# Attention with the maximum subtracted in SBUF, exponentials taken out of the PSUM of the transposes, and scores of two heads as a pair of 48-row matmuls

## The chip, the cores and the metric

One Trainium2 chip, one core. The metric is the time on the device in microseconds, the median over several runs. The traces shown are of one profiled execution each.

## What is computed

A transformer layer over a batch of 8 with 512 positions and 256 channels, all in float32: cross attention from `x` to `ctx` with 16 heads of 16 channels, an additive bias of 512 x 512 that all heads and batches share, and a padding mask; then a feed-forward layer whose weights and activations are rounded block by block to FP4.

```python
q = (query @ w_q.T + b_q).reshape(B, T, H, D)            # query = layernorm(x)
k = (key @ w_k.T + b_k).reshape(B, S, H, D)              # key = value = ctx
v = (value @ w_v.T + b_v).reshape(B, S, H, D)
scores = jnp.einsum('bthd,bshd->bhts', q * SCALING, k) + attn_bias[None]
scores = jnp.where(key_padding_mask[:, None, None, :], NEG_INF, scores)
attn = jax.nn.softmax(scores, axis=-1)
out = jnp.einsum('bhts,bshd->bthd', attn, v).reshape(B, T, E)
x = x + (out @ out_proj_w.T + out_proj_b)
gate = fp4_linear(layernorm(x), w_gate); y = fp4_linear(layernorm(x), w_up)
x = x + fp4_linear(jax.nn.silu(gate) * y, w_down)
```

## The kernel before, in words

The attention is cut into tiles of 128 queries x 512 keys of one head. A batch has 64 tiles, in two octets (periods) of 8 heads; all batches together have 512. The order of the work on each engine is written out by hand: `body(b)` issues a batch, the first and the last batch are unrolled and the others run in a hardware loop, and the engines meet through semaphores only.

A tile passes these stations:

- TensorE makes the scores (L1099). Query and key are split into a high and a low part in fp32r, so that a full-precision product is a single matmul with 128 contraction rows: `stack` holds high and low parts of two heads on top of each other. One head of the pair is zeroed in the query by `parity4`. The scores go to one of three PSUM banks; the matmul waits until VectorE has emptied the bank (`biased`).
- VectorE adds bias and mask, copies to `prob` in SBUF, and takes the row maximum (L845, `neg_max`).
- ScalarE takes the exponential in SBUF with the maximum as its bias and sums the row (L569).
- TensorE transposes the four 128 x 128 blocks (L967, `transpose_prob`) six tiles later, into one of three other banks.
- VectorE (L764, even tiles) or ScalarE (L608, odd tiles) copies the transposed tile to `probT`.
- TensorE multiplies with the values (L1056, `values`): four heads at once in four column groups of 32, eight instructions for one chunk of 128 keys, after every second tile on average.
- The sums are inverted, expanded on GpSimd (L445), transposed (`make_r`, L1002), copied (L614), and multiplied into the output (L733).

Between the tiles TensorE also makes q, k, v and the output projection (L982, L988, L995, L1013) for the next octet or the batch before, and transposes of `xn` and `ctx`. The SP queue copies high and low parts into `stack`, 32 DMAs for each octet (L367, L378), reloads the bias for every batch (L407), and loads the feed-forward weights in the last batch. These weights are quantised in nine pieces during the last batch by VectorE (L808 to L823), GpSimd (L484 to L493), TensorE (L1027, L1030) and ScalarE (L592 to L597). The feed-forward layer then runs over 32 row tiles (L1217 to L1245), after a start in which the last output projection is made. It isn't changed.

## Time and profile before

| | |
|---|---|
| median of 3 runs | 1028.66 us (1028.31 to 1029.89) |
| the profiled execution | 1029.46 us, its span 1027.5 us |
| granted TensorE clock, mean | 0.983 |
| instructions | 23032 |
| PE, DVE, ACT, POOL busy | 93%, 83%, 70%, 19% |

PE is TensorE's matmuls, PEld its weight loads, DVE VectorE, ACT ScalarE, POOL GpSimd, SP the queue that issues the DMAs. The profiled execution took 1.96 us more than its span, and 0.80 us more than the median. A view of the chain follows the work that ended last backwards and gives each piece only the time that nothing earlier covers.

### The profile page before, as it was taken

How to read it: one execution, taken by the hardware profiler on the slowest of the kernel's cores; microseconds unless marked ns; L12 is line 12 of the kernel's file. 1: busy time of each engine (PE TensorE's matmuls, PEld its weight loads, DVE VectorE, ACT ScalarE, POOL GpSimd, SP SyncE). 2: the span in 40 equal slices, each digit the busy share in tenths (PEclk: the TensorE clock that was granted, in tenths of full speed). 3: DMA queues.
4: the chain of work that ended last, by engine and by line, in shares of the span. 5: the costliest groups of instructions: out<-in, count | busy, mean ns of one | idle time of the engine just before them, and what ended most of it. 6: DMA issues, size and time to landing. Idle time of an engine off the chain costs nothing.

```text
span 1027.5 us, 23032 instructions
## 1 busy us (share of the span) xinstructions
PE 952.6 (93%) x6612; PEld 667.7 (65%) x6612; DVE 857.5 (83%) x2125; ACT 722.0 (70%) x1685; POOL 198.6 (19%) x156
## 2 busy tenths in 40 slices
PE   5299999999999999999999999978778999999997
PEld 3176666666657666665765766645456878878885
DVE  3287988888888888888888878899757999999996
ACT  2298988877888888888788888856634555555542
POOL 3222232140240213114024121245400000000000
PEclk9699999999999999999999999999979999999999
DMA  9553451451533335055153433611000000000000
GB/s 290 134 124 76 113 124 27 121 138 28 120 101 90 84 103 123 15 129 132 36 115 93 103 75 89 145 35 31 2 0 6 17 16 15 21 16 15 20 16 26
DMA packets 47339, 76.14 MB, mean 74 GB/s; under 512 B 10016, under 2 KB 26784, under 8 KB 47264
## 3 DMA queue, kind: packets, MB, share of 16 engines
q1 hardware_dynamic: 47264, 75.34, 29.3%
q8 instruction: 22, 0.36, 0.2%
q14 instruction: 53, 0.43, 0.2%
HBM read 20.78 MB, written 4.19 MB: 24 GB/s over the span
## 4 chain that ended last, share of the span: by engine, by line
PE 82%; DVE 8%; issue 5%; SPq 2%; ACT 2%; DMA 1%; DVEq 1%; POOL 0%; ACTq 0%; POOLq 0%
PE psum L967 24%; PE psum L1099 14%; PE psum L1056 12%; PE psum L1235 9%; PE psum L1217 4%; PE psum L1219 4%; PE psum L1218 4%; PE psum L988 3%; PE psum L995 3%; PE psum L1013 2%; PE psum L982 2%; DVE att L845 2%; DVE att L764 2%; SPq L367 1%; SPq L378 1%
## 5 line engine op out<-in xcount | busy, mean ns | idle before, releaser
L569 ACT ACTIVATE att<-att,neg_max 128x512 f32<-128x512 f32 x512 | 367.3, 719 | 119.1 <-DVE neg_max L845 111.9
L845 DVE CUSTOM_DVE_ANT_0 att<-psum,att 128x512 f32<-128x512 f32 x512 | 346.7, 686 | 106.2 <-PE psum L1099 94.2
L967 PE MATMUL psum<-ident,att 128*128 128x128 f32 x2448 | 364.7, 275 | 19.9 <-DVE att L764 7.4
L967 PEld LDWEIGHTS psum<-ident,att 128*128 128x128 f32 x2448 | 298.0, 141 | 94.6 <-issue 45.6
L1099 PE MATMUL psum<-stack 128*128 128x512 f32 x512 | 273.1, 535 | 26.4 <-DMA stack<-kl 17.3
L1099 PEld LDWEIGHTS psum<-stack 128*128 128x128 f32 x512 | 96.7, 189 | 141.4 <-DVE neg_max L845 81.3
L764 DVE COPY att<-psum 128x512 f32<-128x512 f32 x256 | 175.6, 686 | 3.7 <-PE psum L967 3.7
L1056 PE MATMUL psum<-att 128*32 128x256 f32 x2048 | 164.0, 393 | 2.0 <-issue 2.0
L608 ACT ACTIVATE att<-psum 128x512 f32<-128x512 f32 x256 | 150.5, 588 | 18.1 <-PE psum L967 13.1
L1235 PE MATMUL psum<-att 128*128 128x256 f32 (+1 forms) x384 | 98.0, 388 | 2.8 <-ACT att L649 2.8
L569 ACT ACTIVATION_READ_ACCUMULATOR att<-att,neg_max 128x1 f32 x512 | 96.9, 189 | 0.0
L1217 PE MATMUL psum<-stack,qh 128*128 128x512 f32 (+1 forms) x192 | 76.6, 399 | 7.7 <-DVE att L899 7.2
L1235 PEld LDWEIGHTS psum<-att 128*128 128x128 f32 (+1 forms) x384 | 65.7, 189 | 20.1 <-issue 10.6
L654 ACT ACTIVATE att<-psum 128x704 f32<-128x704 f32 x32 | 24.4, 762 | 73.4 <-PE psum L1219 73.4
L473 POOL TENSOR_TENSOR att<-att 128x512 f32<-128x512 f32 x32 | 40.2, 1281 | 179.3 <-DMA att<-in_fside_1xSxS_dram 179.3
L1219 PE MATMUL psum<-stack,ql 128*128 128x512 f32 (+1 forms) x192 | 73.5, 383 | 0.0
L1218 PE MATMUL psum<-stack,qh 128*128 128x512 f32 (+1 forms) x192 | 73.3, 382 | 0.0
L1056 PEld LDWEIGHTS psum<-att 128*32 128x32 f32 x2048 | 40.9, 108 | 45.1 <-issue 43.5
L1217 PEld LDWEIGHTS psum<-stack,qh 128*128 128x128 f32 x192 | 37.2, 194 | 16.6 <-issue 9.0
L464 POOL TENSOR_TENSOR ql<-att,qh 128x1024 fp32r<-128x1024 f32 x16 | 38.0, 2375 | 27.8 <-DVE qh L705 27.7
L845 DVE DVE_READ_ACCUMULATOR2_ANT neg_max<- 128x1 f32 x512 | 42.6, 83 | 0.0
L1218 PEld LDWEIGHTS psum<-stack,qh 128*128 128x128 f32 x192 | 37.4, 195 | 5.8
(96 smaller groups left out, 1043.7 us busy)
## 6 DMA issues: line engine op xcount, KB each, us to landing
stack<-qh SPq DMA_DIRECT2D x128, 128.0 KB, 2.4
stack<-ql SPq DMA_DIRECT2D x128, 128.0 KB, 2.3
att<-in_fside_1xSxS_dram SPq DMA_DIRECT2D x16, 512.0 KB, 3.7
stack<-kh SPq DMA_DIRECT2D x128, 64.0 KB, 2.0
stack<-kl SPq DMA_DIRECT2D x128, 64.0 KB, 2.0
att<-in_ctx_dram SPq DMA_DIRECT2D x8, 512.0 KB, 4.8
out_dram<-att SPq DMA_DIRECT2D x32, 128.0 KB, 1.7
x<-in_x_dram SPq DMA_DIRECT2D x1, 3584.0 KB, 20.4
```

Source lines behind the costliest of these rows:

```text
L473: pool.tensor_tensor(bias_m[:, tt, :], bias_m[:, tt, :], mask_neg, ALU.add).then_inc(bias_ready, 1)
L569: act.activation(prob[:, slot, :], prob[:, slot, :], ACT.Exp, bias=neg_max[:, slot:slot + 1], scale=-1.0, accum_out=row_sum[:, o, tt * 8 + ...
L608: act.activation(probT[:, u % 2, k, :, (tt % 2) * P:(tt % 2) * P + P], ps_T[:, bank_of(jm)[0], :].rearrange("p (c t) -> p c t", c=SC), ACT ...
L764: dve.tensor_copy(probT[:, u % 2, k, :, (tt % 2) * P:(tt % 2) * P + P], ps_T[:, bank_of(jm)[0], :].rearrange("p (c t) -> p c t", c=SC)).th ...
L845: dve.tensor_tensor_reduce(out=prob[:, slot, :], in0=ps_score[:, bank_of(j)[0], :], in1=bias_m[:, tt, :], scale=-1.0, scalar=BIG, op0=ALU. ...
L967: return pe.transpose(out_, in_, ident[:, :])
L1056: last = pe.matmul(ps_O[32 * k:32 * k + 32, half * 2 * P:(half + 1) * 2 * P], vpad[:, o, c, 2 * k + r, :], probT[:, u % 2, k, c, :], start ...
L1099: pe.matmul(ps_score[:, bank, :], q_stack[o][:, k, r, tt * P:(tt + 1) * P], k_stack[o][:, k, :], start=True, stop=True).then_inc(score_rea ...
L1217: pe.matmul(ps_gu[:, c0:c1], f_xqT_high[:, par, c, :], w_gu_high[:, c, c0:c1], start=c == 0, stop=False)
L1218: pe.matmul(ps_gu[:, c0:c1], f_xqT_high[:, par, c, :], w_gu_low[:, c, c0:c1], start=False, stop=False)
L1219: last = pe.matmul(ps_gu[:, c0:c1], f_xqT_low[:, par, c, :], w_gu_high[:, c, c0:c1], start=False, stop=c == EC - 1)
L1235: last = pe.matmul(ps_y[:, 1 - par, :], f_hqT[0:rows, 1 - par, c, :], w_dnT[0:rows, c, :], start=c == 0, stop=c == IC - 1)
```

## The change

The attention is rewritten; the feed-forward loop stays.

- A step is now two tiles, of two heads (r = 0, 1), and `stack` holds 48 rows for each head: high, high, low of the query against high, low, high of the key (`planes_q`, `planes_k`). The 48-row matmuls of a pair stand at rows 0 and 64 of the array. The rows get there through a DRAM tensor, `qk_planes`: 6 DMAs write the planes of an octet and 8 read them, where 32 copied within SBUF.
- The exponential no longer reads `prob`. GpSimd (`less_max`, L548) subtracts the maximum from 20 of the 32 tiles of an octet, ScalarE (L682) from the other 12. The tile is then transposed, and ScalarE's exponential is the copy out of PSUM (L675) for every tile. VectorE has no copy out any more, and no row sums are read.
- The transposes have two banks, one for each r, where they had three, and start four steps (8 tiles) after the scores.
- The sums come from a column of ones beside each head's 16 values (`vv`). The output is copied (`take_O`), transposed to queries in rows (`make_ot`), divided (`normalise`), and transposed back (`make_oT`).
- q, k, v and the output projection are issued in pieces of 256 columns, one a step (`heavy`); transposes stand at the end of a step (`light`).
- The weights' pieces begin with `w_down`; VectorE's work on them starts in step 2 of the last batch's 32 instead of at tile 22 of its 64.

```diff
+        N_OCT = 2 * B
+        STEPS = 16
+        TILES = 2 * STEPS
+        T_LAG = 4
+        V_LAG = 8
+        RING = 16
+        VW = D + 1
...
+        ps_score, ps_O = psum[:, 0:3, :], psum[:, 6, :]
+        ps_T = (psum[:, 3, :], psum[:, 7, :])
+        M0, M1 = psum[:, 4, :], psum[:, 5, :]
...
+        def by_act(s, r):
+            return r == 1 and s % 4 != 0
...
+            def less_max(n, s, r):
+
+
+                slot = (2 * s + r) % RING
+                pool.wait_ge(biased, TILES * n + 2 * s + r + 1)
+                pool.tensor_tensor(prob[:, slot, :], prob[:, slot, :], neg_max[:, slot:slot + 1].to_broadcast([P, S]),
+                                   ALU.subtract).then_inc(less_pool, 1)
...
-                    act.activation(prob[:, slot, :], prob[:, slot, :], ACT.Exp, bias=neg_max[:, slot:slot + 1], scale=-1.0,
-                                   accum_out=row_sum[:, o, tt * 8 + 2 * k + r:tt * 8 + 2 * k + r + 1]).then_inc(exp_ready, 1)
...
+                act.activation(probT[:, u % 2, 2 * kk + r, :, (tt % 2) * P:(tt % 2 + 1) * P], ps_T[r].rearrange("p (c t) -> p c t", c=SC),
+                               ACT.Exp, scale=1.0 if by_act(s, r) else -1.0).then_inc(exp_ready, 1)
...
-                    pe.matmul(ps_score[:, bank, :], q_stack[o][:, k, r, tt * P:(tt + 1) * P], k_stack[o][:, k, :],
-                              start=True, stop=True).then_inc(score_ready, 1)
...
+                for r in range(2):
+                    rows = slice(64 * r, 64 * r + 48)
+                    pe.matmul(ps_score[:, SCORE_BANK[2 * S_ + r], :], q_stack[rows, 2 * o + h, kk, tt * P:(tt + 1) * P],
+                              k_stack[rows, 2 * o + h, kk, :], start=True, stop=True).then_inc(score_ready, 1)
...
+                t = TILES * n + 2 * s + r
+                wait(pe, exp_ready, t - 1)
+                pe.wait_ge(less_act if by_act(s, r) else less_pool, taken_off(n, s, r))
...
+                for S_ in range(2 * STEPS):
+                    scores(b, S_)
+                    transpose_tile(b, S_, 0)
+                    heavy(b, S_, 0)
+                    transpose_tile(b, S_, 1)
+                    values(b, S_)
+                    heavy(b, S_, 1)
+                    light(b, S_)
```

TensorE, in the middle of a batch, before: scores (L1099) of one tile, transposes (L967) of another, and a group of values (L1056) after every second tile.

```order
L1056 MATMUL psum<-att 32x256 x4
L260 REGISTER_ALU
L1099 MATMUL psum<-stack 128x512
L260 REGISTER_ALU
L967 MATMUL psum<-ident,att 128x128 x4
L260 REGISTER_ALU
L1099 MATMUL psum<-stack 128x512
L967 MATMUL psum<-ident,att 128x128 x4
L1056 MATMUL psum<-att 32x256 x4
```

The same place in the change: the pair of scores (L1178), transposes (L1085) of two tiles with a piece of the output projection (L1140) between them, the values (L1214), and at the end of some steps four more transposes.

```order
L1178 MATMUL psum<-stack 128x512 x2
L1188 REGISTER_ALU
L1085 MATMUL psum<-ident,att 128x128 x4
L1140 MATMUL psum<-att 128x256
L1188 REGISTER_ALU
L1085 MATMUL psum<-ident,att 128x128 x4
L1214 MATMUL psum<-att 32x256 x4
L1124 REGISTER_ALU
L1085 MATMUL psum<-ident,att 128x128 x4
L270 REGISTER_ALU x2
```

The two scores of a step moved together and are followed by transposes at once; the number of transposes and of value matmuls for two tiles is the same.

The SP queue, from the load of the rest of `x` to the first octet's operands, before:

```order
L336 DMA x<-in_x_dram 128x28x256
L367 DMA stack<-qh 32x1024 x8
L367 DMA stack<-ql 32x1024 x8
L378 DMA stack<-kh 32x512 x8
L378 DMA stack<-kl 32x512 x8
```

And in the change, where the first four of the eight loads of `stack` are enough for the first eight steps:

```order
L373 DMA x<-in_x_dram 128x28x256
L399 DMA qk_planes<-k_hl 8x16x512 x3
L399 DMA qk_planes<-q_hl 8x16x512 x3
L421 DMA stack<-qk_planes 48x2x512 x8
L399 DMA qk_planes<-q_hl 8x16x512 x3
```

32 issues became 14, and the loads wait for the planes to have been written.

GpSimd in the last batch of the change: a piece of the weights is three instructions (L555, L557, L560) between those of `less_max` (L548).

```order
L548 TENSOR_TENSOR att<-att,neg_max 128x512 x3
L555 TENSOR_TENSOR att<-att 128x512
L557 TENSOR_TENSOR att<-att 128x512
L560 TENSOR_TENSOR att<-att 128x512
L548 TENSOR_TENSOR att<-att,neg_max 128x512 x2
```

The pieces stood alone there before; now tiles of the attention queue behind them.

## Rows read from the trace of the kernel before

**Rows 1.** The page: busy time of each engine, share of the span, instructions

```profile
PE 952.6 (93%) x6612; PEld 667.7 (65%) x6612; DVE 857.5 (83%) x2125; ACT 722.0 (70%) x1685; POOL 198.6 (19%) x156
```

**Rows 2.** Stages: start:end, length, busy PE, PEld, DVE, ACT, POOL, granted clock

```profile
204.63:290.70 86.07, 84.74 (x672) 56.39 (x664) 72.31 (x196) 72.26 (x174) 20.63 (x15) 1.00 0.38 93
635.10:735.30 100.20, 85.03 (x649) 53.99 (x649) 93.21 (x246) 71.13 (x169) 42.49 (x35) 1.00 0.23 59
735.30:748.30 13.00, 10.21 (x101) 5.51 (x99) 5.08 (x14) 6.60 (x16) 1.92 (x2) 0.92 0.01 1
748.30:788.60 40.30, 28.17 (x111) 22.41 (x110) 27.04 (x66) 15.66 (x32) 1.29 (x2) 0.82 0.00 1
```

**Rows 3.** Chain within a middle batch: start, own time, engine, target, line

```profile
413.70 0.24 PE psum L1099
413.94 0.44 PE psum L967 x4
414.38 0.57 PE psum L1056 x8
414.95 0.43 PE psum L1099
...
417.49 0.59 PE psum L967 x4
...
421.72 0.87 PE psum L1013 x4
```

**Rows 4.** Chain within the feed-forward loop, from one down projection to the transposes

```profile
819.91 1.30 PE psum L1235 x6
...
821.33 1.49 PE psum L1235 x6
822.82 0.81 PE psum L967 x6
```

**Rows 5.** PE, 800 to 1000, by shape: busy, mean ns, idle before

```profile
L1235 PE MATMUL psum<-att 64*128 64x256 f32 x50 | 17.4, 428 | 0.0
```

**Rows 6.** Chain at the loop's turn to its next batch

```profile
204.63 2.03 issue
```

**Rows 7.** Groups of one middle batch, by shape: busy, mean ns, idle before, releasers

```profile
L569 ACT ACTIVATE att<-att,neg_max 128x512 f32<-128x512 f32 x64 | 45.9, 719 | 11.4 <-DVE neg_max L845 10.5
L845 DVE CUSTOM_DVE_ANT_0 att<-psum,att 128x512 f32<-128x512 f32 x64 | 43.4, 686 | 12.2 <-PE psum L1099 10.5 <-issue 0.6
...
L608 ACT ACTIVATE att<-psum 128x512 f32<-128x512 f32 x33 | 19.4, 588 | 2.1 <-PE psum L967 1.4
...
L473 POOL TENSOR_TENSOR att<-att 128x512 f32<-128x512 f32 x4 | 5.0, 1284 | 24.7 <-DMA att<-in_fside_1xSxS_dram 24.7
```

**Rows 8.** Timeline of the start: start, duration, engine, line

```profile
20.75 5.06 SPq L367 DMA_DIRECT2D stack<-qh  x8
...
36.08 4.95 SPq L378 DMA_DIRECT2D stack<-kl  x8
...
42.57 1.19 PE L1099 MATMUL psum<-stack 128*128 128x512 f32 x2 [17.34 <-DMA stack<-kl]
```

**Rows 9.** DMA issues, 18 to 42: KB each, us to landing

```profile
stack<-qh SPq DMA_DIRECT2D x8, 128.0 KB, 5.4
```

**Rows 10.** Waits in the last batch: total us, times, longest

```profile
PEld psum L1099 <- DVE neg_max L845: 17.0, 26, 2.3
```

**Rows 11.** Chain near the end of the last batch

```profile
728.79 0.47 DVE stack L796
...
729.86 0.60 DVE att L845
```

**Rows 12.** GpSimd, 635 to 750, by shape: busy, mean ns, idle before

```profile
L486 POOL TENSOR_TENSOR att<-att 128x512 f32<-128x512 f32 x9 | 11.5, 1281 | 0.7
```

**Rows 13.** Timeline of ScalarE where the feed-forward layer starts

```profile
745.47 0.60 ACT L614 ACTIVATE att<-psum 128x512 f32<-128x512 f32 x1 [2.44 <-PE psum L967]
745.96 0.50 ACT L636 ACTIVATE att<-x,neg_mean 128x256 f32<-128x256 f32 x1
```

More of the change, by code:

```diff
@@ L48, in xattn_ffn @@
     SC = S // P
-    TILES = 32
-    UNIT = 8
     ROWS = B * NT
@@ new lines, in planes_free, with bias_again @@
+            def planes_free(o, loads):
+                for h in range(2):
+                    sp.wait_ge(stacked[2 * o + h], 64 * loads)
+                    plain(sp)
+            planes_k(0)
+            planes_q(0)
+            stack_octet(0, 0)
+            planes_free(0, 1)
+            planes_q(1)
+            def bias_again(b, tt):
+                sp.wait_ge(biased, b * 2 * TILES + TILES + 2 * (8 + 2 * tt + 2))
+                plain(sp)
+                sp.dma_start(bias_m[:, tt, :], bias_v[:, tt, :]).then_inc(bias_in[tt], 16)
@@ new lines, in make_tc, with make_qk @@
+            def make_tc(bp, i, bank):
+                pe.wait_ge(ctx_in, 16 * (bp + 1))
+                for tt in range(NT):
+                    last = transposes(bank[:, tt * P:(tt + 1) * P], ctx_n[:, tt, i * P:(i + 1) * P])
+                last.then_inc(tc_ready, 1)
+            def make_qk(which, o, piece, bank, ready):
+                h, c = piece // 2, piece % 2
+                src = (xnT, ctxT)[which]
+                cols = slice(h * 2 * P, (h + 1) * 2 * P)
+                last = pe.matmul(bank[:, cols], w_inT[:, c, which * E + o * P:which * E + (o + 1) * P], src[:, c, cols],
+                                 start=c == 0, stop=c == EC - 1)
+                if piece == 3:
+                    last.then_inc(ready, 1)
@@ L998, in make_v, with make_ot @@
+            def make_v(i, piece, bank):
+                x, c = piece // 2, piece % 2
+                s = 2 * i + x
+                last = pe.matmul(bank[:, x * E:(x + 1) * E], ctxT[:, c, s * P:(s + 1) * P], w_inT[:, c, 2 * E:3 * E],
+                                 start=c == 0, stop=c == EC - 1)
+                if piece == 3:
                     last.then_inc(v_ready, 1)
-            def make_r(n):
-                pe.wait_ge(inv_ready, n + 1)
+            def make_ot(quad, bank):
+                pe.wait_ge(O_taken, quad + 1)
@@ new lines, in make_ot, with make_oT, make_out @@
+                last.then_inc(ot_ready, 1)
+            def make_oT(m, o, bank):
+                pe.wait_ge(ot_taken, 2 * m + 2)
+                for tt in range(NT):
+                    last = transposes(bank[:, tt * P:(tt + 1) * P], O_n[:, tt, o * P:(o + 1) * P])
+                last.then_inc(oT_ready, 1)
+            def make_out(i, piece, bank):
+                x, c = piece // 2, piece % 2
+                tt = 2 * i + x
+                last = pe.matmul(bank[:, x * E:(x + 1) * E], oT[:, c, tt * P:(tt + 1) * P], w_outT[:, c, :],
+                                 start=c == 0, stop=c == EC - 1)
+                if piece == 3:
@@ L1196, in step @@
+            batches(pe, body)
+            for S_ in range(V_LAG):
+                transpose_tile(B, S_, 0) if S_ < T_LAG else None
+                transpose_tile(B, S_, 1) if S_ < T_LAG else None
+                values(B, S_)
+                if S_ == 2:
+                    weights_free(8)
+                    make_ot(4 * B - 2, M1)
             def step(n, par):
```

1139 lines of the change are left out of this document (609 added, 530 removed).

## The prediction

> **What bounds the kernel now.** The page comes first: PE is busy 93% of the span, DVE 83%, ACT 70%, POOL 19% [rows 1]. That is an average, so the stages come next. Six middle batches take 86.0 to 86.3 us each, and in one of them PE is busy 84.7 of 86.07 us, DVE and ACT 72.3 [rows 2]. The last batch takes 100.2 us with PE busy only 85.0 and DVE 93.2. Then 13.0 us of drain, and 40.3 us of a start of the feed-forward layer in which PE is busy 28.2 [rows 2]. The first scores start at 42.57 [rows 8].
>
> For the middle batch I read the chain, because it gives each piece its own price. Four transposes cost 0.44 us, a group of values 0.57, a score matmul 0.24 if transposes stand ahead of it and 0.43 if values do. Four transposes behind values cost 0.59 instead of 0.44, and two 256-column projection pieces 0.87 [rows 3]. So two tiles cost 0.24 + 0.44 + 0.43 + 0.44 + 0.57 = 2.12 us, and 32 such pairs 67.8. Projections (32 pieces of 0.435) add 13.9, 24 other transposes at 0.11 add 2.6, and the turn of the loop 2.0 [rows 6]: 86.3 against 86.07 measured. TensorE's order of instructions explains the middle batches by itself. DVE, ACT and POOL are not what is paid for there, however much the change relieves them.
>
> **What a middle batch costs then.** The copy by DVE, the row sums and the exponential in SBUF go. By the prices above they were hidden under PE: 72.3 of 86 us on DVE and ACT. So I cost their removal at nothing, and look at PE alone.
>
> - The pair of scores. Half of the array's rows serve each head. If the two run side by side, the pair costs one matmul behind values: 0.43. No row shows such a pair. The nearest is a group of values: eight instructions in four column groups cost 0.57, much less than eight times a 256-column piece's 0.22 [rows 3]. From that I take the pair as one. The other bound is a second matmul of 0.24.
> - The switch of shape. The pair has 64-row tiles, the transposes behind it the full array. Two rows price this. Six down matmuls of which two have 64 rows cost 1.49 against 1.30, and the six transposes behind them 0.81 against 6 x 0.11 = 0.66 [rows 3 to 5]. So a switch costs 0.15 to 0.19, as 0.59 against 0.44 does behind values. I add 0.15 to the first transposes of each step; the switch in front of the pair is in the 0.43.
> - A step is then 0.43 + 0.59 + 0.44 + 0.57 = 2.03, against 2.12 for the same two tiles. I use 2.04 for the second start.
>
> In the Trainium skill, "TensorEngine Tiling (Array Packing)", section Tiling Modes, changing the tiling mode drains the TensorE, and the 0.15 to 0.19 of the rows agree. By "TensorE: Matmul & The Clock Gate", Part 3, matmuls in different row groups start about 4 ns apart; taken alone that would make the pair one matmul, and no row here shows it.
>
> 32 steps make 65.3. Projections stay at 13.9. Other transposes rise from 24 to 40 (outputs there and back, no sums): 4.4. Ten groups of them stand behind values, with a switch each: 1.5. With the loop's 2.0 the batch costs 87.1, against 86.3 by the same prices: +0.8, or **+5 us** for six batches. The saving on scores is paid out again for switches and transposes.
>
> Are the others fast enough? ACT takes 64 exponentials out of PSUM, from 0.50 (a plain copy's 588 ns less overlap) to 0.62 (the exponential's 719) each, 24 subtractions at 0.62 and 15 copies at 0.5: 54 to 62 of 87 us [rows 7]. POOL subtracts 40 tiles at 1.28, 51 us, plus about 17 for its other work (20.6 now, less the expansions of the sums) [rows 2]: 68. DVE keeps 64 score operations at 0.60 [rows 7, 11] and 14 us of small work (72.3 now, less 64 and 32 operations at 0.60): 52. All have room.
>
> **The start: -10.5 us.** Now 32 issues follow each other from 20.75 to 41.0, 0.63 each, and the first score waits for the last [rows 8]. Then it is six plane writes, whose last issue falls at about 22; a landing of up to 5.4 us beside the load of `x` [rows 9], giving 26 to 27; four loads of `stack` at 0.63, 2.5 us; and 3 us to land, between the 1.5 from the last issue to the first score now [rows 8] and 5.4. First score at about 32; with 5.4 for both landings 35, with 1.5 for both 28.
>
> **The first batch: 0.** It has fewer transposes and values in both kernels. Its first steps are paced by DVE at 1.2 us and more instead of PE; a like excess is in the batch now.
>
> **The last batch: -11 us.** PE without waits: 32 x 2.04 = 65.3, eight value pieces and eight output pieces 7.0, 60 transposes 6.5, 15 switches 2.3: 81. Now it waits 17.0 us for DVE [rows 10], as the weights and the copies meet there. The copies go (32 at 0.60, 19 us), so DVE's sum falls from 93 to 74 to 78. But steps 18 to 28 hold two weight operations each, at 0.47 to 0.60 and more [rows 11], beside 1.2 us of scores, two take-outs and two divisions: about 35 us against 27 on PE, with three score banks and so little lead. That costs 8. POOL is as close: 40 tiles and nine pieces of 3 x 1.28 [rows 12] and small work make 89 to 92 us, of which four steps of lead (9 us) hide most. 81 + 8 = 89 against 100.2.
>
> **Drain and hand-over: +2 us.** Four steps of transposes and values at 1.6 and four of values at 0.45, with the last exponentials: 10 against 13.0 [rows 2]: -3. But ACT may begin the feed-forward layer only after the copy of the last output, while it begins now at 745.96, 2.3 us before the last values end [rows 13]; and the last octet goes through transposes there and back with a copy each (0.44 + 0.6) before its projection: +5.
>
> **The sum**: -10.5 + 0 + 5 - 11 - 3 + 5 = -14.5. Against the profiled execution's 1029.5 (span 1027.5 and 2 around it) that is 1015; that execution lies 0.8 over the median of 1028.66, so 1014.2, I say 1014. The profit per step that decides is small: 14.5 / 256 = 0.057 us. Any price over that on the pair turns the sign.
>
> **The rivals.**
> - The pair runs one after the other. Then each step costs 0.21 to 0.24 more on PE, 54 us for 256 steps, of which the last batch's waits take in 6: 1062, slower. Against it speaks the group of values, in columns only. Chance 0.10.
> - The pair runs side by side, but its second weights (128 columns) load after the first. A load not covered by a matmul shows as 0.43 instead of 0.24, drain and load together, so at most 0.11: 28 us, 1042, slower. Chance 0.08.
> - Two transpose banks are too few. A bank is free only when ACT has done its exponential, with a subtraction of 0.62 and perhaps a copy ahead of it. From T_ready I get about 0.5 + 0.62 + 0.67 = 1.8 us plus the hops, and the next transposes into the bank come 2.04 later, or 2.47 where a projection piece is between. In 28 of 32 steps there is one. If every step still lost 0.07 to 0.1, it would be 2.4 a batch: 19 us, 1033. Chance 0.10.
> - The switch to the pair and back costs nothing extra. 256 x 0.15 = 38 less: 976. The rows with 64-row tiles speak against it. Chance 0.06.
> - The sum holds: 0.66, with a range of its own from 1000 to 1028 (start ±3, last batch -4 to +8, middle batches ±0.8 each, hand-over ±3).
>
> **How the numbers follow.** The time is that of the sum. From 990 to 1044 lie the last case's range, the third case, nearly all of the second, and what lies between: 0.8. A measurement of this kernel tells 0.2%, 2 us, from no change. Faster than 1026.6: 0.61 of the 0.66, all of the fourth case's 0.06, and 0.03 of the third: 0.70. Within 0.2%: 0.05. Slower: 0.25.
>
> **What would show it.** In the changed trace: the two score matmuls start within some 10 ns, and the chain has about 0.43 for both; transposes behind them at 0.59, not 0.44; a middle batch at 86 to 88 us with PE busy nearly all of it; the first score near 32; VectorE's share of the middle batches near 60%; a last batch near 89, with waits for DVE and POOL. Score matmuls 0.2 apart would make the prediction wrong, and so would PE waiting for the exponential in ordinary steps.

## The result, and the profile after

The changed kernel takes **1049.87 us** (median of 4 runs, 1044.90 to 1052.12), the kernel before 1029.28 beside it (1028.31 to 1031.17): a ratio of 1.0191, 95% interval 1.0152 to 1.0231. It is slower, by 1.9%. I had forecast 1014 and "faster" at 0.70; the time lies outside my range of 990 to 1044 as well. The profiled execution is the slowest of the four, 2.25 us over the median, so the sum by stages below explains 22.7 us of span where the medians differ by 20.6.

The page of the changed kernel, whose profiled execution took 1052.12 us (compare [rows 1]; the columns are those of the page):

```profile
span 1050.2 us, 22498 instructions
PE 965.9 (92%) x6740; PEld 651.1 (62%) x6740; DVE 725.6 (69%) x1897; ACT 604.7 (58%) x1125; POOL 501.1 (48%) x478
...
L675 ACT ACTIVATE att<-psum 128x512 f32<-128x512 f32 x512 | 303.7, 597 | 258.4 <-PE psum L1085 257.8
L548 POOL TENSOR_TENSOR att<-att,neg_max 128x512 f32<-128x512 f32 x320 | 338.9, 1066 | 233.0 <-DVE neg_max L949 230.6
L1085 PE MATMUL psum<-ident,att 128*128 128x128 f32 (+1 forms) x2576 | 406.8, 285 | 18.6 <-DMA att<-in_ctx_dram 13.9
```

The work moved as planned: VectorE has 132 us less, ScalarE 117 less, GpSimd 302 more, TensorE 13 more. Nothing there looks like 22.7 us of span. So the stages again: start:end, length, busy time (and number) of PE, PEld, DVE, ACT and POOL, granted clock, DMA share, GB/s. The borders are the first score of each batch, the last score step, and the first matmul of the feed-forward layer.

```profile
0.00:39.35 39.35, 12.92 (x66) 11.53 (x66) 7.31 (x18) 7.33 (x11) 14.44 (x22) 0.83 0.83 250
39.35:126.36 87.01, 79.09 (x558) 47.74 (x558) 53.22 (x164) 50.35 (x90) 56.23 (x54) 0.90 0.46 100
126.36:211.78 85.42, 84.92 (x686) 53.25 (x682) 54.06 (x167) 57.75 (x104) 57.82 (x56) 1.00 0.42 94
211.78:301.78 90.00, 86.55 (x684) 54.24 (x680) 54.45 (x167) 57.73 (x104) 57.84 (x56) 0.98 0.40 89
573.58:658.85 85.27, 84.93 (x685) 53.25 (x681) 50.23 (x155) 57.75 (x104) 54.19 (x52) 1.00 0.41 95
658.85:753.75 94.90, 80.94 (x650) 49.62 (x647) 88.48 (x216) 54.91 (x101) 81.63 (x72) 0.98 0.21 55
753.75:772.14 18.39, 12.01 (x122) 7.18 (x123) 5.66 (x18) 11.13 (x22) 4.01 (x4) 0.95 0.00 1
```

Of the six middle batches the first and the last take 85.4 and 85.3 us, and the second 90.0; the three left out, of the same kind as the second, take 89.7 to 91.1. What these four have and the two don't is a turn of the loop (the branch back to the start of its body), which falls between their first and their second step on TensorE. The sum against the trace of before, by the same borders (first scores there at 42.57, 119.41 and 634.19, last step at 734.95, feed-forward layer from 750.82): start -3.2, first batch 87.0 against 76.8, +10.2 (the batch ahead of the loop); the six middle batches 532.5 against 514.8, +17.7; last batch 94.9 against 100.8, -5.9; drain and hand-over 18.4 against 15.9, +2.5; the rest +1.4. That is +22.7.

### The profile page after: what moved, and what is told of

The parts are those of the page before. It is cut to its first block and busy times, and to the rows that moved or that the text cites. A ratio compares the mean times of both kernels' runs of the same rounds, so it can differ in the third digit from the quotient of the medians.

```text
span 1050.2 us, 22498 instructions
## 1 busy us (share of the span) xinstructions
PE 965.9 (92%) x6740; PEld 651.1 (62%) x6740; DVE 725.6 (69%) x1897; ACT 604.7 (58%) x1125; POOL 501.1 (48%) x478
## 5 line engine op out<-in xcount | busy, mean ns | idle before, releaser
L675 ACT ACTIVATE att<-psum 128x512 f32<-128x512 f32 x512 | 303.7, 597 | 258.4 <-PE psum L1085 257.8
L548 POOL TENSOR_TENSOR att<-att,neg_max 128x512 f32<-128x512 f32 x320 | 338.9, 1066 | 233.0 <-DVE neg_max L949 230.6
L1085 PE MATMUL psum<-ident,att 128*128 128x128 f32 (+1 forms) x2576 | 406.8, 285 | 18.6 <-DMA att<-in_ctx_dram 13.9
L1085 PEld LDWEIGHTS psum<-ident,att 128*128 128x128 f32 (+1 forms) x2576 | 295.1, 143 | 146.0 <-issue 88.4
L1178 PE MATMUL psum<-stack 48*128 48x512 f32 x512 | 131.2, 508 | 40.1 <-DVE neg_max L949 22.9
L1214 PE MATMUL psum<-att 128*32 128x256 f32 x2048 | 164.9, 395 | 0.2 <-ACT att L675 0.2
L682 ACT ACTIVATE att<-att,neg_max 128x512 f32<-128x512 f32 x192 | 138.0, 719 | 22.7 <-DVE neg_max L949 22.7
L1178 PEld LDWEIGHTS psum<-stack 48*128 48x128 f32 x512 | 49.3, 187 | 128.4 <-DVE neg_max L949 66.9
L1417 PE MATMUL psum<-stack,q_hl 128*128 128x512 f32 (+1 forms) x192 | 76.3, 397 | 7.1 <-DVE att L1015 7.0
L1107 PE MATMUL psum<-att 128*128 128x256 f32 x256 | 76.1, 388 | 1.0 <-DVE att L930 1.0
L1419 PE MATMUL psum<-stack,q_hl 128*128 128x512 f32 (+1 forms) x192 | 73.4, 382 | 0.0
L1418 PE MATMUL psum<-w_gu_low,q_hl 128*128 128x512 f32 (+1 forms) x192 | 73.2, 381 | 0.0
L1214 PEld LDWEIGHTS psum<-att 128*32 128x32 f32 x2048 | 40.8, 108 | 44.2 <-issue 38.4
L1417 PEld LDWEIGHTS psum<-stack,q_hl 128*128 128x128 f32 x192 | 37.2, 194 | 16.0 <-issue 8.1
L1117 PE MATMUL psum<-att 128*128 128x256 f32 x128 | 42.9, 420 | 0.0
L1418 PEld LDWEIGHTS psum<-w_gu_low,q_hl 128*128 128x128 f32 x192 | 37.2, 194 | 5.7
## 6 DMA issues: line engine op xcount, KB each, us to landing
x<-in_x_dram SPq DMA_DIRECT2D x1, 3584.0 KB, 17.7
```

The source lines that it names most:

```text
L548: pool.tensor_tensor(prob[:, slot, :], prob[:, slot, :], neg_max[:, slot:slot + 1].to_broadcast([P, S]), ALU.subtract).then_inc(less_pool, 1)
L675: act.activation(probT[:, u % 2, 2 * kk + r, :, (tt % 2) * P:(tt % 2 + 1) * P], ps_T[r].rearrange("p (c t) -> p c t", c=SC), ACT.Exp, scal ...
L682: act.activation(prob[:, slot, :], prob[:, slot, :], ACT.Identity, bias=neg_max[:, slot:slot + 1], scale=-1.0).then_inc(less_act, 1)
L1085: return pe.transpose(out_, in_, ident[:, :])
L1107: last = pe.matmul(bank[:, cols], w_inT[:, c, which * E + o * P:which * E + (o + 1) * P], src[:, c, cols], start=c == 0, stop=c == EC - 1)
L1178: pe.matmul(ps_score[:, SCORE_BANK[2 * S_ + r], :], q_stack[rows, 2 * o + h, kk, tt * P:(tt + 1) * P], k_stack[rows, 2 * o + h, kk, :], st ...
```

## The experiments

**Is the pair side by side?** The timeline of TensorE in a middle batch of the changed kernel: start, duration to the end of the last of a group, line, name, number.

```profile
301.45 0.40 PE L1214 MATMUL psum<-att 128*32 128x256 f32 x4
301.78 0.50 PE L1178 MATMUL psum<-stack 48*128 48x512 f32 x2
302.21 0.66 PE L1085 MATMUL psum<-ident,att 128*128 128x128 f32 x4
302.71 0.60 PE L1117 MATMUL psum<-att 128*128 128x256 f32 x2
```

Two score matmuls of 512 columns, and the transposes follow 0.43 us behind the start of the first. The two of a pair start 3 to 4 ns apart, in all 256 pairs of the trace. The run that parts them (`e8_unpaired`):

```diff
...
-                    scores(b, S_)
+                    scores(b, S_, 0)
                     transpose_tile(b, S_, 0)
+                    scores(b, S_, 1)
                     heavy(b, S_, 0)
```

> The changed kernel with the second score matmul of each pair moved behind the first four transposes: the same instructions, not side by side any more. My theory (side by side, the second matmul of a pair costs 4 ns; alone it costs 0.43 behind transposes with a switch of shape there and 0.15 back, less 0.0 hidden): each step rises from 2.04 to about 2.5 or 2.6, 256 steps of 0.5 make 120 to 148 us, about 1170 to 1200. The pair-serial rival: the same matmul costs the same wherever it stands, and only the two switches of 0.15 are added: 77 us or less, below 1127.

1172.26 us (1.1381, 1.1362 to 1.1400). A middle batch takes 104.41 us with PE busy for all of it, 19.1 more than 85.27, or 0.60 a step. In its timeline the single score stands 0.42 to 0.43 ahead of what follows:

```profile
302.96 0.66 PE L1085 MATMUL psum<-ident,att 128*128 128x128 f32 x4
303.55 0.49 PE L1178 MATMUL psum<-stack 48*128 48x512 f32 x1
303.97 0.70 PE L1140 MATMUL psum<-att 128*128 128x256 f32 x2
304.51 0.60 PE L1085 MATMUL psum<-ident,att 128*128 128x128 f32 x4
```

From start to start, the second score takes 0.42, the transposes ahead of it 0.59 instead of 0.50, and the piece of projection behind it 0.54 instead of 0.43: in this step 0.42 for the matmul itself and 0.2 for the two extra changes of shape. One matmul and a pair cost the same, so the first rival (one after the other) and the second (weights that load late) are out.

**The turn of the loop.** First without any loop (`e1_unroll`, the edit shown), and the same in the kernel before (`e2_before_unroll`):

```diff
-            body(0)
-            with eng.Fori(1, B - 2) as b:
+            for b in range(B):
                 body(b)
-            body(B - 2)
-            body(B - 1)
```

> The changed kernel with its loop over the middle batches written out: eight bodies in a row, no branch, nothing else. In its trace the batches with a loop turn behind them take 89.7 to 91.1 us and the two without one 85.3 and 85.4. Theory A (the turn of the loop is what the middle batches lose: VectorE stands 5.6 us there, TensorE 3 us behind it, and the granted clock then falls to half for some us): every middle batch near 85.4, no stretch at half clock between 75 us and the last batch, so five times 4.6 to 5.7 less: 23 to 28 us off 1049.9, about 1024. Theory B (the steps themselves cost more, and the turn only shows where it adds up): the loop's own 2 us go five times, 10 us, about 1040. Rival C (the turn's loss is a data wait that stays without a branch): less than 5 us off.

> The control: the kernel before with its loop written out in the same way. There VectorE stands 2.9 us at the turn and the clock stays at full speed, and the batches with a turn differ from the one without by 2.0 us. Both theories: about six times 2.0, 12 us off 1029, about 1018. If it gains as much as the changed kernel does from the same edit (some 25 us), the turn isn't what makes the changed kernel slower; if it gains 10 to 12, then the turn accounts for about 13 us of the 20 between the kernels.

The changed kernel took 1034.56 us (1.0040, 1.0016 to 1.0064; 1028.05 to 1038.27), 15 less and between the two theories; the kernel before 1018.29 (0.9896, 0.9873 to 0.9919), 11 less. The loops have four and five turns, not the five and six that I had counted. One middle batch of each, the changed kernel first:

```profile
295.10:380.37 85.27, 84.93 (x684) 53.29 (x680) 53.88 (x167) 57.67 (x104) 57.78 (x56) 1.00 0.41 94
```

```profile
202.84:286.96 84.12, 84.12 (x665) 56.38 (x665) 72.18 (x196) 72.55 (x174) 20.96 (x16) 1.00 0.40 96
```

All six are alike to 0.02 us in either kernel. This parts two effects: the steps cost 1.15 us more a batch (I had 0.8), 6.9 in all; and a turn costs 1.9 to 2.2 in the kernel before (five turns, 10.1 us), 4.4 to 5.8 in the changed one (four turns, 20.7). The trace of before shows its turn too, if each batch is counted from its first score: the first middle batch, with no turn ahead of it, takes 84.07 us, the other five 86.03 to 86.30. The profiled execution is 24 us shorter than that with the loop; the median gained only 15. The profiled one with the loop was the slowest of its four, the one without it the fastest of its ten, and those ten fall into two groups: four of 1028.05 to 1029.35 with mean clocks of 0.975 to 0.978, six of 1034.29 to 1038.27 with 0.964 to 0.970. Why isn't settled.

At the turn VectorE stands still. Its timeline in the changed kernel: the last operation ahead of the turn, and the first behind it.

```profile
301.27 0.08 DVE L949 DVE_READ_ACCUMULATOR2_ANT neg_max<- 128x1 f32 x1
306.61 0.69 DVE L949 CUSTOM_DVE_ANT_0 att<-psum,att 128x512 f32<-128x512 f32 x1 [5.26 <-issue]
```

SP had issued three plane writes 2 to 4 us ahead, and TensorE's next scores wait:

```profile
297.03 2.13 SPq L399 DMA_DIRECT2D qk_planes<-q_hl  x3
...
307.37 0.80 PE L1178 MATMUL psum<-stack 48*128 48x512 f32 x2 [3.05 <-DVE neg_max L949]
```

And then the clock is down, by stretches of 3 us (columns as above):

```profile
304.00:307.00 3.00, 0.31 (x8) 0.00 (x0) 0.39 (x1) 1.18 (x3) 0.00 (x0) 0.87 0.16 55
307.00:310.00 3.00, 2.63 (x9) 1.91 (x10) 2.49 (x8) 0.60 (x1) 2.61 (x3) 0.50 0.00 0
310.00:313.00 3.00, 3.00 (x17) 1.42 (x16) 0.32 (x2) 0.60 (x1) 3.00 (x3) 0.50 0.32 69
313.00:316.00 3.00, 3.00 (x26) 1.91 (x25) 1.31 (x4) 1.69 (x3) 1.11 (x2) 0.99 0.51 193
```

After 3 us in which TensorE stood, it is granted 0.50 (1.2 instead of 2.4 GHz) for 6 us of work. The four turns differ in this: TensorE stood 2.6 to 3.05 us at each, and the granted clock was 0.50 for 6.8 us at the two whose batches take 91.1 us, for 3.4 us at the two of 89.7 and 90.0. The kernel before has a clock of 1.00 in all its middle batches.

**Do the plane writes do it?** Two runs move them behind the turn. In `e3_planes_after_turn`:

```diff
-            planes_free(0, 1)
-            planes_q(1)
...
             def body(b):
+                sp.wait_ge(biased, b * 2 * TILES + 4)
...
+                planes_free(0, b + 1)
+                planes_q(2 * b + 1)
...
                     bias_again(b, 2)
-                    planes_free(0, b + 2)
-                    planes_q(2 * b + 3)
                     bias_again(b, 3)
```

> The changed kernel keeps its loop, but the three writes of the query planes (256 KB each) that it issues at the end of a body, 2 to 4 us ahead of the turn, are issued early in the next body. Theory A1 (VectorE's fetch of its instructions after the branch lands late because it stands beside these writes and the loads around them): VectorE's stand at the turn falls from 5.6 us to the 2.9 of the kernel before or less, the clock stays up, and the batches with a turn come to 87 to 88: 10 to 18 us off, 1032 to 1040. Rival A2 (the stand is the longer body's own: more code to fetch, whatever the transfers do): 5.6 us stay, the time stays within 3 us of 1049.9, or it gets worse if the second half's planes then come late.

1083.98 us (1.0529, 1.0494 to 1.0564), 34 slower than the changed kernel, where I had expected 10 to 18 less. Its waits of TensorE in one batch name what took the place of the turn:

```profile
PE psum L1084 <- DMA att<-in_ctx_dram: 4.2, 1, 4.2
```

TensorE's gap at the turn is down to 0.2 to 0.5 us, with as long a body as before; but SP now comes to the context load only 22.6 us into the batch, behind the plane writes and eight stack loads; TensorE stands for it 3.2 to 4.4 us in each of these batches. They take 91.4 to 92.6 us, and the last one 103.7. `e5_planes_and_ctx` puts the context load first in the body, ahead of `planes_q`.

> The changed kernel with its loop, where the next context load, in every batch but the last, is the first transfer that SP issues in a body, and the query plane writes come behind it instead of ahead of the turn. In the run that moved the plane writes alone, the gap of TensorE at the turn was gone (no stand over 1 us there, 2.8 to 3.4 us before), and one of 3.8 to 4.4 us for the context load stood in its place about 28 us into each batch. Theory A1 (two places in SP's queue that exclude each other: plane writes ahead of the turn delay VectorE's instructions, plane writes behind it delay the context tile): with the context load ahead both stands go, batches with a turn take 87 to 88, the first one 79 to 81: 18 to 24 us off 1049.9, 1026 to 1032. Rival (the context tile is late because the stacks and planes keep the DMA engines busy, wherever it is queued): a stand of 2 us or more stays in each batch and the time stays above 1045.

1032.45 us (1.0038, 1.0021 to 1.0056). The loop is still there, and the turn has nearly no price, 0.4 to 0.6 us: here 85.84 us against 85.27 unrolled.

```profile
289.51:375.35 85.84, 85.00 (x685) 53.24 (x682) 54.58 (x167) 57.67 (x104) 57.77 (x56) 1.00 0.39 93
632.08:734.24 102.16, 82.67 (x650) 50.46 (x647) 89.28 (x216) 54.92 (x101) 81.42 (x72) 0.95 0.22 56
```

The last batch pays 7.3 us back: the feed-forward weights come behind the plane writes in the queue, and VectorE waits for the first of them:

```profile
DVE att L908 <- DMA att<-in_L_ffn_w_down_dram: 7.6, 1, 7.6
```

**Traffic, or the order of waits?** Transfers of no use are put back at the old place, in the kernel of `e5_planes_and_ctx` (`e13_copies_at_turn` with three, `e16_six_copies` with six) and in the kernel before (`e14_before_copies` with three, `e17_before_six` with six):

```diff
+                for i in range(3):
+                    sp.dma_start(copy_no[i], bias_v[:, i, :]).then_inc(copied, 16)
```

> The changed kernel with the context load first and the plane writes after the turn (that run: 1032.45, batches with a turn 85.7 to 85.8), and in addition three transfers of 256 KB each at the place where the plane writes had stood, 3 to 4 us ahead of VectorE's branch. They copy rows of the bias in DRAM to a spare DRAM tensor that nothing reads. Theory A1 (transfers in flight when VectorE branches delay its instruction fetch): its stand at the turn is back at 4 us or more, TensorE stands 1.5 us or more, and batches with a turn take 88 to 91: 10 to 25 us slower than without the copies. Rival (the stand came from the order of waits around the plane writes, not from traffic): batches stay at 85.7 to 86.3 and the time within 3 us of 1032.45.

> The kernel before with the same three copies in each batch but the last, issued about 3 us ahead of its turn. There VectorE stands 2.7 us at a turn and the batches take 86.0 to 86.3, against 84.1 without a turn. Theory A1: the stand rises to 4.5 us or more and the six batches with a turn to 88 to 91, the clock falls there too: 10 to 25 us slower than 1029. Rival: unchanged within 3 us.

1033.98 and 1034.61 us (1.0061, 1.0036 to 1.0087; 1.0054, 1.0034 to 1.0073). The first is the rival's number, 1.5 us more than without copies; the second, 5.8 us over the kernel before, is neither's (VectorE stands 3.4 to 4.2 us at its turns instead of 2.5 to 2.7). But in the changed kernel three copies, from DRAM to DRAM, are soon over: in the turn where VectorE's last operation ends at 289.67 us, the DMA view has 0.01 MB from 289.6 to 290.4. Behind the last operation in the changed kernel it has 0.56 MB from 301.4 to 304.3. So twice as many copies:

> As the run with three copies ahead of the turn in the changed kernel (context load first, plane writes after the turn; 1033.98 there, 1032.45 without copies), but with six. Refined theory A1 (the instruction packets come when the data queued ahead has passed): the first packet comes at 3 to 4.5 us behind the branch, VectorE stands 4.0 us or more instead of 1.9 to 2.7, TensorE 1.5 us or more, and batches with a turn take 88 to 91: 1041 to 1055. Rival: the stand stays below 3 us and the time within 4 us of 1034.

> As the run with three copies ahead of the turn in the kernel before (1034.61; VectorE stood 2.9 to 3.7 us at its turns instead of 2.0 to 2.2), but with six. Theory A1: first packet at 3 to 5 us behind the branch, a stand of 4.5 to 6 us, batches of 89 to 92 and a clock that falls at some turns: 1043 to 1065. Rival: below 1037.

1048.13 us (1.0170, 1.0153 to 1.0187) and 1041.83 (1.0106, 1.0088 to 1.0123); the batches with a turn take 87.7 to 91.5 and 88.0 to 88.6, the second kernel a little under what I expected. Copies that nobody needs bring the loss back: by the medians 15.7 us over the run without them in the changed kernel, 11.7 in the kernel before (13.6 and 10.9 by the ratios). The half clock comes back with them in both kernels: it is granted for 3.4 us behind every turn of the kernel before, where without copies it never was. VectorE's turn with six copies in the changed kernel, and the turn without any (`e5_planes_and_ctx`) behind it:

```profile
292.76 0.08 DVE L962 DVE_READ_ACCUMULATOR2_ANT neg_max<- 128x1 f32 x1
297.21 0.69 DVE L962 CUSTOM_DVE_ANT_0 att<-psum,att 128x512 f32<-128x512 f32 x1 [4.36 <-issue]
```

```profile
289.00 0.08 DVE L952 DVE_READ_ACCUMULATOR2_ANT neg_max<- 128x1 f32 x1
291.63 0.69 DVE L952 CUSTOM_DVE_ANT_0 att<-psum,att 128x512 f32<-128x512 f32 x1 [2.55 <-PE psum L1088]
```

The DMA view of these turns (queue: packets, MB, share of 16 engines) says what is late: the first packet of q14, a queue that carries instructions. In the changed kernel, from 300.6 to 304.3 us there are only data, and from 304.3 to 304.8 comes the packet:

```profile
q1 hardware_dynamic: 374, 0.70, 62.0%
```

```profile
q1 hardware_dynamic: 35, 0.07, 36.7%
q14 instruction: 1, 0.01, 3.9%
```

With six copies, from 292.8 to 294.9, again only data; the packet comes at 294.96:

```profile
q1 hardware_dynamic: 67, 0.54, 79.8%
```

Without copies, from 289.1 to 289.6, it comes at once and with no data beside it:

```profile
q14 instruction: 1, 0.01, 6.4%
```

VectorE goes on 2.2 to 2.6 us behind the first packet at all 16 turns of the four runs of the changed kernel (as it was, `e5`, `e13`, `e16`), however late the packet is. In the kernel before there are two packets, and it goes on 2.3 to 2.5 us behind the second, 2.7 to 3.1 with three copies. (The release by PE that the row of `e5` names is the latest event that the profile knows of.) That the packets of q14 are VectorE's code is inferred from this timing.

**The first batch.** In the changed kernel SP issues the next context load at 59.74 us, behind the key planes and eight stack loads; in the kernel before it was the first load of the body, at 41.15. `e4_ctx_early` issues it ahead of them, in the first batch only:

```diff
+                if is_first(b):
+                    ctx_again()
                 planes_k(2 * b + 1)
                 stack_octet(2 * b + 1, 1)
                 if not last:
-                    sp.dma_start(ctx_n[:, :, :], ...)
+                    if not is_first(b):
+                        ctx_again()
```

> The changed kernel, where in the first batch alone the load of the first context tile is issued ahead of the writes of the key planes and the stack loads instead of behind them. In its trace TensorE stands 5.9 us at 63 us for that load. Theory: the stand goes, the clock that falls to half after it stays up, and the first batch takes 79 to 81 us instead of 87.0: 6 to 8 us off 1049.9. Rival: the load is late for the traffic beside it, not for its place in the queue: then the stand stays at 3 us or more and the gain is below 3 us.

1044.39 us (1.0143, 1.0118 to 1.0167): 5.5 less. Its first batch takes 79.25 instead of 87.01, the 5.5 us in which TensorE's matmuls stood are gone (5.9 is the gap of its weight loads), and with them the half clock behind them (0.50 from 69.0 to 74.1 in the changed kernel). The kernel before takes 76.84; the 2.4 us that are left weren't looked into, but there the half clock of the start ends 3.8 us after the first score (46.4), and in this run 12.2 us after it (51.2).

**The start.** `e6_start_split`:

```diff
-            sp.dma_start(x1[:, NT:ROWS, :], x_v[:, NT:ROWS, :])
+            sp.dma_start(x1[:, NT:2 * NT, :], x_v[:, NT:2 * NT, :])
...
             planes_free(0, 1)
+            sp.dma_start(x1[:, 2 * NT:ROWS, :], x_v[:, 2 * NT:ROWS, :])
...
+                            dve.wait_ge(xrest_in, 32)
```

> The changed kernel with the load of the last three quarters of x split: batch 1's rows stay where they are, the other 1.5 MB or so is issued behind the first stack loads. In the trace of the changed kernel the plane writes, issued by 22.8, landed only at 32.2 while that load ran. Theory D (the x load beside them is what makes the plane writes late): planes land by 27, first score at 32 to 34 instead of 39.35, and 5 to 8 us off 1049.9. Rival (plane writes of 768 KB take this long by themselves): the first score stays within 2 us of 39.35. It may also show whether the half clock of the first 11 us of scores moves with the first score or stays at its time.

The part moved is 3 MB, not 1.5. It took 1054.75 us (1.0250, 1.0221 to 1.0280), 4.9 more than the changed kernel where I had expected 5 to 8 less. SP's queue at the start, the changed kernel first:

```profile
20.27 2.52 SPq L399 DMA_DIRECT2D qk_planes<-q_hl  x3
32.35 3.65 SPq L421 DMA_DIRECT2D stack<-qk_planes  x8
```

```profile
19.75 4.34 SPq L399 DMA_DIRECT2D qk_planes<-q_hl  x3
29.07 3.66 SPq L421 DMA_DIRECT2D stack<-qk_planes  x8
```

The planes land 5.0 us after their last issue instead of 9.6, and the first score comes at 35.97: half of the gain that I expected. The rest lies in the second hop, 6.9 to 7.0 us from the first stack load to the first score in either kernel. The context load then stands behind `x`: TensorE waits 12.2 us for it, and the first batch takes 93.5. The half clock at the start ends at 49.0 us (50.2 in the changed kernel), so it lies over the first 13.1 us of the scores instead of 10.9.

**The last batch.** VectorE's groups, kernel before and after (busy, mean ns; `L821` became `L918`, `L817` `L914`, `L823` `L920`, `L808` `L905`, `L811` `L908`):

```profile
L817 DVE TENSOR_TENSOR att<-att 128x512 f32<-128x512 f32 x9 | 6.2, 684 | 0.0
L808 DVE TENSOR_REDUCE att<-att 128x32 f32<-128x512 f32 x9 | 6.1, 678 | 0.0
...
L823 DVE TENSOR_SCALAR att<-att 128x512 f32<-128x512 f32 x9 | 4.2, 465 | 0.3
L821 DVE TENSOR_SCALAR att<-att 128x512 uint32<-128x512 uint32 x9 | 3.7, 412 | 0.0
```

```profile
L914 DVE TENSOR_TENSOR att<-att 128x512 f32<-128x512 f32 x9 | 9.8, 1085 | 0.1
L918 DVE TENSOR_SCALAR att<-att 128x512 uint32<-128x512 uint32 x9 | 8.7, 965 | 0.1
L920 DVE TENSOR_SCALAR att<-att 128x512 f32<-128x512 f32 x9 | 7.4, 826 | 0.3
L905 DVE TENSOR_REDUCE att<-att 128x32 f32<-128x512 f32 x9 | 6.1, 677 | 0.0
```

The same operations on the same shapes are 1.6 to 2.3 times longer, except the reduction and those that read PSUM. `e7_pool_narrow` shrinks GpSimd's subtractions in the last batch to 8 columns and leaves the other 504 as they are, so the attention of that batch isn't the reference's:

```diff
+                w = 8 if isinstance(n, int) and n >= 2 * B - 2 else S
-                pool.tensor_tensor(prob[:, slot, :], ...
+                pool.tensor_tensor(prob[:, slot, 0:w], ...
```

> The changed kernel, where GpSimd's subtractions in the last batch cover only 8 of 512 columns of a tile (the rest of those tiles isn't subtracted, so the last batch's attention isn't the reference's). Semaphores and order are the same, but GpSimd is busy some 25 us instead of 70 in the last batch. Theory E (VectorE's SBUF-to-SBUF operations are lengthened by GpSimd working in SBUF at the same time: the 512-column ones took 965, 1085 and 826 ns where the kernel before has 412, 684 and 465): they fall back to within 10% of those, VectorE's sum in the last batch from 88.5 to about 75, and the last batch from 94.9 to 87 to 90, which is what I had forecast. Rival (they are longer because of what ScalarE or PSUM does): they stay above 750 and the batch stays above 93. Second rival (they shorten, but the last batch is held by the placing of the weight pieces against the scores): they shorten and the batch stays above 92.

1043.73 us (1.0144, 1.0100 to 1.0189). VectorE's groups and the batch there:

```profile
L915 DVE TENSOR_TENSOR att<-att 128x512 f32<-128x512 f32 x9 | 6.8, 757 | 0.1
...
L919 DVE TENSOR_SCALAR att<-att 128x512 uint32<-128x512 uint32 x9 | 4.6, 516 | 0.1
L921 DVE TENSOR_SCALAR att<-att 128x512 f32<-128x512 f32 x9 | 3.8, 427 | 0.3
```

```profile
653.68:742.84 89.16, 80.58 (x651) 49.70 (x648) 78.72 (x216) 54.70 (x101) 49.24 (x74) 0.98 0.23 58
```

Two of the three come within 11% of the kernel before and the integer one at 25% over it. The 32-column operation (358 ns before, 592 after) didn't shorten, 615 here, so its cause is another, which I didn't look for. VectorE has 9.8 us less (I had expected about 13), and the batch 5.7: 89.16, the 89 of the forecast. The edit also makes GpSimd itself quicker, but little of the gain comes that way: TensorE's waits for VectorE (`neg_max`) fall from 9.6 to 5.9 us, that for a piece of weights from GpSimd from 3.2 to 2.3. GpSimd's pieces of weights are still there.

**Put together.** `e9_unroll_ctx` is the unrolled kernel with the early context load, `e10_unroll_ctx_start` adds the split of `x`; `e11_unroll_ctx_half` and `e12_all_three_half` are these two with `by_act` as `return r == 1` (32 and 32 tiles); `e15_all_three_48` has `r == 1 or s % 2 == 1` (48 for ScalarE, 16 for GpSimd).

> The changed kernel with its loop written out and, in the first batch, the context load issued ahead of the key plane writes and stack loads. The two edits took 15.3 and 5.5 us off alone, and act at different places (turns of the middle batches, a 5.9 us stand in the first batch). If they add: 1049.9 - 15.3 - 5.5 = 1029, and by the profiled executions (batches of 85.27 instead of 90, first batch 79.25 instead of 85.12, last batch 94.7) 1026.3 - 5.9 + 1.8 = 1022. The execution-to-execution spread of the unrolled kernel (1028 to 1038) should shrink to 3 us if its cause is the 4.2 us stand in the first batch. Against the kernel before it would be faster or the same; against that kernel with its own loop written out (1018) slower still, by the 1.15 us per batch that the steps cost.

> As the kernel with the loop written out and the early context load, with the load of x split as well. Alone the split brought the first score from 39.35 to 35.97 and lost 6.4 us in the first batch, since the context load then stood 12.2 us behind x. Theory: with the context load ahead of the key planes only part of that stays, as x (1.5 MB in this split, and more) is still issued ahead of it: 0 to 3 us better than without the split if the context tile is in time, 2 to 6 us worse if TensorE stands for it at 60 us again.

> As the kernel with the loop written out and the early context load, with ScalarE subtracting 32 of a batch's 64 tiles instead of 24, and GpSimd 32 instead of 40. Theory E (GpSimd's work lengthens VectorE's SBUF-to-SBUF operations in the last batch; with GpSimd's subtractions nearly gone the batch fell from 94.9 to 89.2): a fifth of GpSimd's subtractions less gives about a fifth of that, 1 to 1.5 us off the last batch, and VectorE's 512-column integer operation from 965 to 850 to 900 ns. Middle batches stay at 85.3 if ScalarE (58% busy) has room: 8 x 0.72 = 5.8 us more for it of 85. Rival: ScalarE's exponential then comes late in the steps with a copy as well, and batches rise by 0.5 or more each, 3 us or more slower in all.

> All of these together: loop written out, early context load, split load of x, subtractions halved between ScalarE and GpSimd. If the effects add, it is the run with the split plus the difference that the halving makes without it; nothing else is expected.

> The changed kernel with loop written out, early context load, split load of x, and ScalarE subtracting 48 of a batch's 64 tiles, GpSimd 16 (32 and 32: 1023.24; 24 and 40: 1025.08). Theory E: VectorE's 512-column operations of the last batch come near those of the kernel before (the integer one from 965 to 650 to 750 ns), the last batch goes from 94.7 to 91 to 92. ScalarE then has 38 + 34 + 8 = 80 of 85.3 us in a middle batch. Rival: that is too much for it, its exponentials come late, and the middle batches rise over 86: slower than 1025.

| kernel | median | ratio to before, 95% | first batch | middle | last |
|---|---|---|---|---|---|
| e9_unroll_ctx | 1026.89 | 0.9967 (0.9951 to 0.9983) | 79.20 | 85.27 | 98.53 |
| e10_unroll_ctx_start | 1025.08 | 0.9956 (0.9940 to 0.9972) | 79.93 | 85.27 | 94.68 |
| e11_unroll_ctx_half | 1024.07 | 0.9944 (0.9926 to 0.9962) | 80.12 | 85.27 | 93.89 |
| e12_all_three_half | 1023.24 | 0.9931 (0.9913 to 0.9949) | 79.53 | 85.28 | 95.09 |
| e15_all_three_48 | 1032.69 | 1.0025 (1.0012 to 1.0039) | 83.67 | 87.00 | 90.05 |

The times of the stages are those of one execution each. The first kernel is 2 us under the sum of the two edits' medians. The spread didn't shrink to 3 us as expected (1022.48 to 1029.87), so the stand in the first batch isn't all of its cause; the last batch of that profile and of the fourth had a clock of 0.93, the others 0.96 to 0.98. The split of `x` costs nothing once the context load is early, but gains only 2 us, within the spread.

The halving changed no middle batch, and took VectorE's integer operation from 965 to 842 ns in the profile with the split; at 48 tiles it is at 421, the last batch at 90.05, but ScalarE is busy 71 of 87 us, TensorE's weight loads wait 6.5 us a batch for exponentials, and each middle batch is 1.7 us longer: the rival won there. The operation with two inputs (`L914`, 1085 ns) stayed at 1115 and 1049 in the two, so how much each operation suffers doesn't follow GpSimd's subtractions alone. `e12_all_three_half` beats both kernels; the kernel before with its loop written out beats it, by the ratios of 0.9896 and 0.9931 (the intervals just meet, but its four runs, 1017.30 to 1019.51, lie below the four of the other, 1020.03 to 1024.62).

## Why the prediction was wrong

The step that failed first is one that I hadn't priced as part of the change: "the loop's 2.0 the batch costs 87.1". That 2.0 was right for the kernel before, and the changed kernel's turns cost 4.4 to 5.8. Point by point, by the traces:

- **The steps: right.** A pair of scores at 0.43; two transpose banks that make TensorE wait 0.3 us in a whole batch of `e1_unroll`. From start to start the four pieces of a step take 0.43, 0.49, 0.53 and 0.57, 2.02 in all; the sum had 0.43, 0.59, 0.44 and 0.57, so its total is right and its split between the two groups of transposes isn't. That gives 85.27 and 85.42 us without a turn against my 85.1 (87.1 less 2.0). The unrolled kernels put the difference at 1.15 a batch against the 0.8 of the sum.
- **The turn: wrong, 12.7 us** of the six middle batches (+17.7 measured, +5 forecast; 2 of them the steps). I took 2.0 for it as a property of the loop, and as part of all six middle batches: counted from first score to first score, the first of them takes 84.07 us and not "86.0 to 86.3". What a turn costs depends on what SP has in flight: the change puts 768 KB of plane writes 2 to 4 us ahead of the branch. Moving them takes the loss away, and six copies in their place bring it back, in both kernels. That it works through the fetch of VectorE's instructions is inferred. That TensorE then runs at half clock made a stand of 3 us into a loss of 4.4 to 5.8.
- **The first batch: wrong, 10.2 us** where I said 0. I had followed engines only, and not SP's queue, in which the context load, first in the body before, now stands behind key planes and 8 stack loads. Moving it gives 7.8 of them back in the profile, 5.5 by the medians.
- **The start: 7.3 us short** (-3.2 for -10.5). Planes at 32.3 instead of 26 to 27, which the load of `x` explains to the extent of 3.3 to 4.6 us; and 6.9 us for the stack loads where the sum had 5.5.
- **The last batch: 5 us short** (-5.9 for -11). The term that was mis-sized is VectorE's "74 to 78": it is 88.5, since I priced its weight operations as they were, with GpSimd busy 42% of the batch instead of 86%. With GpSimd's subtractions narrowed VectorE's sum is 78.7 and the batch 89.16. (The 17.0 us of [rows 10] are waits of weight loads; the matmuls waited 8.4. The sum didn't use them.)
- **Drain and hand-over: right** (+2.5 for +2). The hand-over is visible as TensorE's 5.5 us from the last values to the first matmul of the layer (2.5 before). Its two parts weren't measured apart.

These make 12.7 + 10.2 + 7.3 + 5.1 + 0.5 and 1.4 of the rest, which nothing here explains: the 37.2 between -14.5 and +22.7. None of my rivals was the one that came: their doubt lay on TensorE's pair and its banks, and none of it on the transfers.

The Trainium skill, "TensorE: Matmul & The Clock Gate", Part 3, has matmuls of different row groups start about 4 ns apart. The trace agrees: 3 to 4 ns in each of its pairs, and `e8_unpaired` shows what the pair saves, 0.60 us a step.

## What to carry to other kernels

When a change turns one kind of transfer into another, follow the DMA queue through a whole loop body as closely as the engines: what stands behind the new transfers, and what is in flight when an engine branches. The turn of a loop had no constant price here: it cost 0.4 to 5.8 us, with the traffic of the moment and the clock that TensorE lost while it stood. GpSimd's new work in SBUF made some of VectorE's operations longer, so a sum of busy time from before came out too low. And write the loop out once as a measurement, in both kernels: it parts the cost of the steps from that of the turns at once, and here it made the kernel before 11 us faster.

## What the hardware showed

- VectorE's stand at a loop turn follows the data in flight. Behind its last operation the first packet of the instruction queue came after 0.2 us with idle DMA engines (`e5`), 2.1 to 3.1 us with six copies (`e16`), 2.5 to 3.0 with the plane writes; the stand was 2.4 to 2.6, 4.4 to 5.4 and 4.8 to 5.3 us.
- Three of VectorE's operations from SBUF to SBUF on 512 columns took 412, 465 and 684 ns in the last batch with GpSimd busy 42% of it, 965, 826 and 1085 with GpSimd busy 86%. The reduction (678 and 677) and the score operation, which reads PSUM (684 and 679), didn't change.
- TensorE that stood 3.05 us at the turn was then granted 0.50 of its clock for 6 us; in the unrolled kernel the middle batches have a clock of 1.00 throughout.
- The spread of 7 to 10 us between runs of the unrolled changed kernel stays unexplained: `e1` in two groups with mean clocks of 0.975 to 0.978 and 0.964 to 0.970, `e9` with 0.972 to 0.980. The kernel before, unrolled, spreads by 2.
